# Layer 0 of a two-layer graph network: destination rows added to source rows by accumulating gathers into the message buffers

## What is computed

```python
s_n, v_n = _equiv_layernorm(s, v, gamma_s, beta_s, gamma_v)
src, dst = (edge_index[0], edge_index[1])
msg_s = (s_n @ Ws_src)[src] + (s_n @ Ws_dst)[dst]
msg_v = jnp.einsum('ncx,cd->ndx', v_n, Wv_src)[src] + jnp.einsum('ncx,cd->ndx', v_n, Wv_dst)[dst]
y0, y1 = (rsh[:, 0], rsh[:, 1:4])
w1 = rbf @ W_rbf
m1_s, m1_v = _cg_tp(msg_s, msg_v, y0, y1, w1[:, :CS], ...)
a = (m1_s @ W_alpha).reshape(e, H, AS_)
...
agg = jax.ops.segment_sum(alpha * h, dst, num_segments=n)
```

## Time and profile before

| what | value |
|---|---|
| median of 3 runs | 10095.94 us (10092.63 to 10127.31) |
| span of the profiled execution, first to last instruction | 8679.9 us |
| median less this span | 1416.0 us |
| layer 0's edge loop in the trace, from its first gather | 301 to about 6050 us |
| its regular groups (all but the first three and the last 26) | 380 to 5468 us |

### The profile page before, as it was taken

The page is one execution under the profiler, slowest core; times in us unless marked ns, Lnnn a source line. Parts: engine busy times, 40 slices in busy tenths (PEclk is TensorE's granted clock), DMA queues, the critical chain, the costliest instruction groups (busy, mean ns, idle before and its releaser), DMA issues. The chain is left out here.

```text
span 8679.9 us, 218293 instructions
## 1 busy us (share of the span) xinstructions
PE 7627.6 (88%) x60373; PEld 5771.5 (66%) x60374; DVE 7274.4 (84%) x17597; ACT 3252.4 (37%) x8375; POOL 6016.9 (69%) x5890
## 2 busy tenths in 40 slices
PE   2599999999999999999999999887968888888888
PEld 1487777877877787877787778776644444444445
DVE  4699999999999999999999999775368888888886
ACT  1244444444444444444444444332222222222223
POOL 0477777777777777777777777651037777777774
PEclk9799999999999999999999999987569999999999
DMA  4344444444444444444444444321012222222222
GB/s 53 78 101 99 102 100 101 102 100 101 101 102 101 101 101 99 102 100 100 100 101 102 101 102 100 77 75 29 11 37 67 67 67 67 67 67 67 67 67 61
DMA packets 616622, 725.52 MB, mean 84 GB/s; under 512 B 284132, under 2 KB 390884, under 8 KB 616573
## 3 DMA queue, kind: packets, MB, share of 16 engines
q0 software_dynamic: 225408, 385.00, 20.4%
q1 hardware_dynamic: 391165, 339.92, 15.3%
HBM read 708.40 MB, written 16.06 MB: 83 GB/s over the span
## 5 line engine op out<-in xcount | busy, mean ns | idle before, releaser
L778 PE MATMUL bank_pair<-w_msg,blocks 128*128 128x160 f32 (+2 forms) x15640 | 2078.7, 288 | 126.8 <-DVE blocks L1030 98.2
L720 POOL DMA_INDIRECT got_src<-src_tab,idx x1564 | 1661.5, 1062 | 659.4 <-POOL idx L714 358.5
L778 PEld LDWEIGHTS bank_pair<-w_msg,blocks 128*128 128x128 f32 x15640 | 1972.7, 192 | 218.5 <-DVE blocks L1030 218.5
L1504 POOL DMA_INDIRECT gotf<-f_tab,idx x1568 | 1702.3, 1086 | 514.2 <-issue 477.4
L720 POOL DMA_INDIRECT got_dst<-dst_tab,idx x1564 | 1486.3, 950 | 528.7 <-issue 503.7
L802 PEld LDWEIGHTS bank_pair<-weights_t,product 128*128 128x128 f32 x12896 | 1498.7, 195 | 309.9 <-issue 295.6
L802 PE MATMUL bank_pair<-weights_t,product 128*128 128x128 f32 x12896 | 1575.5, 281 | 9.5 <-ACT weights_t L932 8.2
L1545 PE MATMUL bank_pair<-val,to_node 128*128 128x385 f32 x3136 | 1247.6, 545 | 5.0 <-DVE val L1659 5.0
L1600 ACT ACTIVATE val<-pre,y_edge 128x160 f32<-128x160 f32 x1568 | 542.8, 417 | 1534.0 <-DVE pre L1640 1531.4
L1545 PEld LDWEIGHTS bank_pair<-val,to_node 128*128 128x128 f32 x3136 | 621.6, 208 | 536.8 <-issue 270.1
L767 PE MATMUL bank_pair<-edge,w_edge 64*128 64x512 f32 x3128 | 884.8, 642 | 9.5 <-DVE blocks L1030 9.5
(11 more groups left out here) (268 smaller groups left out, 11950.3 us busy)
## 6 DMA issues: line engine op xcount, KB each, us to landing
rbf<-in_rbf SPq DMA_DIRECT2D x391, 256.0 KB
dst_bc<-in_dst_rows SPq DMA_DIRECT2D x391, 256.0 KB
y<-in_y SPq DMA_DIRECT2D x391, 128.0 KB
y<-in_y SPq DMA_DIRECT2D x391, 96.0 KB
gotf<-f_tab,idx POOLq DMA_INDIRECT x1568, 2.7
got_src<-src_tab,idx POOLq DMA_INDIRECT x1564
got_dst<-dst_tab,idx POOLq DMA_INDIRECT x1564
rbf<-in_rbf SPq DMA_DIRECT2D x392, 32.0 KB, 1.7
```

The source lines that it names most:

```text
L720: pool.indirect_dma_start(out=buf[slot][:, t, :], out_offset=None, in_=table[:, :], in_offset=bass.IndirectOffsetOnAxis(ap=idx[slot][:, c: ...
L778: return nc.tensor.matmul(to, blocks[rows, k, P * t:P * t + P], w_msg[rows, c0:c1], start=start, stop=stop)
L1504: pool.indirect_dma_start(out=got[k][:, t, :], out_offset=None, in_=f_tab[:, :], in_offset=bass.IndirectOffsetOnAxis(ap=idx[k][:, t:t + 1] ...
```

## The change

The two pairs of gather buffers, POOL's add and its semaphore `summed` are gone. The gathers of the source rows write straight into `msg`. When all four of a group have landed (64 counts of `got`), four gathers of the destination rows follow, with `compute_op` add, so that the DMA engines add what they fetch to what `msg` holds. POOL's step g now does all of this for group g + 2, and `scale_edge(g + 2)` comes behind it. PE waits for all eight gathers (128 counts of `got`) where it waited for `summed`.

```diff
--- before.py
+++ after.py
@@ -505,6 +505,11 @@
     return use if slot == 1 else use - 1
 
 
+def next_use(slot, use):
+
+    return use if slot == 0 else use + 1
+
+
 def group_of(ap, g):
 
     return ap[g] if isinstance(g, int) else ap[bass.ds(g, 1)].squeeze(0)
@@ -514,7 +519,7 @@
         "ident", "iota_col", "least_bc", "idx_all", "w_edge", "w_msg", "w_val", "adot", "psum", "src_tab", "dst_tab",
         "peak", "sums"))
     s = {n: ctx.enter_context(nc.semaphore("l0_" + n)) for n in (
-        "edge0", "edge1", "edge_y0", "edge_y1", "dst0", "dst1", "got0", "got1", "indexed", "summed", "scaled",
+        "edge0", "edge1", "edge_y0", "edge_y1", "dst0", "dst1", "got0", "got1", "indexed", "scaled",
         "turned", "turned_copied", "weighed", "block_done", "message", "message_s", "tanh", "scalars", "leaky", "vector",
         "gated", "logit", "logit_step", "logit_wide", "geometry", "product", "scaled_y", "sum_copied", "projected",
         "far", "logit_turned", "top", "highest", "shifted", "peak_kept", "rescale", "weights", "factors",
@@ -604,8 +609,6 @@
                     chain.end()
 
         idx = [tmp(f"idx{i}", [P, 2 * TILES], I32) for i in range(2)]
-        got_src = [tmp(f"got_src{i}", [P, TILES, D]) for i in range(2)]
-        got_dst = [tmp(f"got_dst{i}", [P, TILES, D]) for i in range(2)]
         msg = [tmp(f"msg{i}", [P, TILES, D]) for i in range(2)]
         edge = [tmp(f"edge{i}", [P, GE]) for i in range(2)]
         y_edge = [tmp(f"y_edge0{i}", [P, TILES, 5]) for i in range(2)]
@@ -714,20 +717,19 @@
                     pool.tensor_copy(idx[slot][:], idx_all[:, bass.ds(g, 1), :].rearrange("p a c -> p (a c)")).then_inc(s["indexed"], 1)
                     wait(s["indexed"], g + 1)
 
-                def gather(slot, tiles):
-                    for t in tiles:
-                        for buf, table, c in ((got_src, src_tab, t), (got_dst, dst_tab, TILES + t)):
-                            pool.indirect_dma_start(
-                                out=buf[slot][:, t, :], out_offset=None, in_=table[:, :],
-                                in_offset=bass.IndirectOffsetOnAxis(ap=idx[slot][:, c:c + 1], axis=0)
-                            ).then_inc(s[f"got{slot}"], 16)
-
-                def add_message(g, slot, use, first):
-                    wait(s[f"got{slot}"], use * 128 + 128)
-                    if not first:
-                        wait(s["turned"], g * 2 - 2)
-                        wait(s["weighed"], g * 4 - 5)
-                    pool.tensor_tensor(msg[slot][:], got_src[slot][:], got_dst[slot][:], ALU.add).then_inc(s["summed"], 1)
+                def gather(slot, table, first, op):
+                    for t in range(TILES):
+                        pool.indirect_dma_start(
+                            out=msg[slot][:, t, :], out_offset=None, in_=table[:, :],
+                            in_offset=bass.IndirectOffsetOnAxis(ap=idx[slot][:, first + t:first + t + 1], axis=0), compute_op=op
+                        ).then_inc(s[f"got{slot}"], 16)
+
+                def take_sources(slot):
+                    gather(slot, src_tab, 0, ALU.bypass)
+
+                def add_targets(slot, use):
+                    wait(s[f"got{slot}"], use * 128 + 64)
+                    gather(slot, dst_tab, TILES, ALU.add)
 
                 def scale_edge(g, slot, use, first):
                     wait(s[f"edge{slot}"], use * 48 + 48)
@@ -739,25 +741,19 @@
                 def step(g, slot, use, now, mid, late):
                     if isinstance(g, int) and g + 2 >= NG:
                         return
-                    further = not (isinstance(g, int) and g + 4 >= NG)
-                    add_message(g + 2, slot, use + 1, False)
-                    if further:
-                        take_idx(g + 4, slot)
-                        wait(s["summed"], g + 3)
-                        gather(slot, (0, 1))
+                    wait(s[f"got{slot}"], use * 128 + 128)
+                    take_idx(g + 2, slot)
+                    wait(s["turned"], g * 2 + 2)
+                    take_sources(slot)
+                    add_targets(slot, use + 1)
                     scale_edge(g + 2, slot, use + 1, False)
-                    if further:
-                        gather(slot, (2, 3))
 
                 for first in range(2):
                     take_idx(first, first)
-                    gather(first, range(TILES))
+                    take_sources(first)
                 for first in range(2):
-                    add_message(first, first, 0, True)
+                    add_targets(first, 0)
                     scale_edge(first, first, 0, True)
-                    take_idx(first + 2, first)
-                    wait(s["summed"], first + 1)
-                    gather(first, range(TILES))
                 schedule(step, 2)(pool)
 
             @block.tensor
@@ -872,7 +868,7 @@
                     if now:
                         message_vectors(3).then_inc(s["message"], 1)
                     if now and not last_group(g):
-                        pe.wait_ge(s["summed"], g + 2)
+                        pe.wait_ge(s[f"got{other}"], next_use(slot, use) * 128 + 128)
                         if mid:
                             pe.wait_ge(s["top"], g)
                         else:
@@ -881,7 +877,7 @@
                         if mid:
                             pe.wait_ge(s["weights_copied"], g)
                         turn_message(other, 1)
-                pe.wait_ge(s["summed"], 1)
+                pe.wait_ge(s["got0"], 128)
                 turn_message(0, 0)
                 turn_message(0, 1)
                 schedule(step)(pe)
```

## The result

| | us, median | ratio to before, 95% interval |
|---|---|---|
| before | 10095.06 (10092.63 to 10127.31, 4 runs) | |
| changed | 11691.41 (11686.12 to 11708.22, 4 runs) | 1.1575 (1.1556 to 1.1594) |

The change costs 1596 us. The number forecast was 11005, the range 10300 to 11900. The time lies in the range, but in the part that the prediction gave to its rival of dear accumulating gathers.

What follows compares the result with a forecast made beforehand. TensorE and DVE were taken as the bound, POOL level with them. POOL's step would go from 14.09 to 16.62 us: +913 over 361 steps, -20 at the start, +15 at the end, +908, about 11005 us; range 10300 to 11900.

Steps and rivals of the forecast that it cites:

- rival of dear accumulating gathers: POOL's adding gathers cost 1.64 us each or delay the sources: step 19.1 us, 11910 us; chance 0.20 for above 11500.
- the landing becomes POOL's own time: POOL, between source and adding gathers: landing exposed at 3.5 us a step, ends 1.6 and 4.5, lengthened by SP's loads.
- the restart of 0.89: POOL after the landing: 0.89 us a step before the first adding gather, as after the copy of the indices.
- one that may join: The 256 KB dst_bc load may join SP's loads beside the source gathers and share the DMA engines.
- the low end taken from layer 1: Quiet landing behind the fourth source gather's row, from layer 1's same gather: 1.6 to 1.75 us.
- the sources and POOL's sum with copying gathers: POOL's step: four source gathers with gaps 4.92 us, the whole step 16.62 us with adding gathers priced as copying ones.
- DVE's line 998: Without POOL's add, DVE's line 998 falls to about 0.26 us on average, freeing 0.8 us of DVE a step.
- the accumulating gather taken at a copying one's price: POOL's adding gathers: 1.005 us each, four with gaps 4.92 us a step; the DMA engines' add priced at nothing.
- a mean over 1.2 us: Sign that the prediction is wrong: the adding gathers' mean on POOL is over 1.2 us.
- the base: Layer 0 step of the kernel before, taken from its first trace: 14.09 us.
- 1416 us around the span: Time outside the 8679.9 us span, taken from the median of the runs and kept beside a new span of about 9590.
- about 3 us before the transposes: TensorE waits for DMA or POOL ahead of its transposes, about 3 us a step, busy share 81% against 96%.

Runs made afterwards that it cites:

- the kernel of copying gathers: Changed kernel with plain destination gathers in place of adding ones, behind the same wait, the sum left out; 10455.82 us, ratio 1.0327.
- the second trace of the kernel before: The kernel before, unchanged, profiled a second time: span 10103.5 us at clock 0.878, 16.42 us a step; measured 10124.48 us, ratio 1.0011.
- the first execution: The kernel before, unchanged, in the trace that the prediction read: span 8679.9 us at an average granted clock of 0.947.
- the edge product in between: Changed kernel with POOL's edge product moved between the source gathers and the adding ones; SP's loads follow it; 10033.15 us, ratio 1.0067.
- second try with late loads: Changed kernel with SP's edge loads, and dst_bc behind them, waiting until the source gathers that POOL issues next have landed; 10362.48 us, ratio 1.0424.
- the accumulating kernel without the wait: Changed kernel with adding destination gathers into separate buffers that nobody reads, no wait for the sources, message the source row alone; 11761.09 us, ratio 1.1625.
- the three kernels of 11761 to 12443 us: Changed order without the wait, destination gathers into separate buffers: accumulating 11761.09 us; copying with POOL's add back 12102.89 us; copying without the sum 12442.46 us.
- 12916: Changed order with plain gathers into two buffer sets, no wait, no POOL add; TensorE sums by two accumulating matmuls per transpose; 12916.21 us, ratio 1.2963.

## Why the prediction came out as it did

**Right: the landing becomes POOL's own time.** The prediction had 4.39 us a step of landing and restart and wrote of 4.4 us as the sign. The changed kernel shows 450.2/97 = 4.64. That SP's loads make it long is shown, too: 4.64 us with them beside the sources, 2.39 with them behind. With the three edge loads beside the sources and `dst_bc` elsewhere, in the kernel of copying gathers, it is 3.1. So the larger part of the lengthening seems to come with `dst_bc`, which the prediction named as one that may join; that kernel has no adding gathers, and the two were not separated. Less the restart of 0.89, the 2.39 are 1.5 us of quiet landing, just under the low end taken from layer 1, 1.6 us.

**Right: the sources and POOL's sum with copying gathers.** Four sources with their gaps are 4 x 0.975 + 3 x 0.315 = 4.85 us, predicted 4.92. The kernel with the wait and without the accumulation goes at 17.4 us a step, of which POOL waits 0.9 us for PE; its own work is about 16.5, where the sum without dear adds, 16.62, stood.

**Right by luck: DVE's line 998.** It is L994 after; its group is 194 in 42.1 us, 259 ns, predicted 0.26. But the reason, that POOL's add is gone, doesn't hold for the timed runs. In the second trace of the kernel before, the add is still there and takes 1544 ns, and the line is as short (2000 to 4000 us):

```profile
L998 DVE SCALAR_TENSOR_TENSOR sums<-sums,factors,win_scaled 128x41 f32 x242 | 52.6, 259 | 28.2 <-DVE win_scaled L991 28.2
```

So the 0.8 us a step that DVE was to gain were there in the first execution only.

**Wrong: the accumulating gather taken at a copying one's price.** This is the step that failed. "The nearest row is that of the plain gather of the same 128 rows, and I take 1.005 us" put the four adds at 4.92 us. They are 4 x 1.927 + 3 x 0.305 = 8.6 us. An undisturbed one is 1.54 to 1.60, some 0.6 us over the copying one, or 2.2 to 2.4 us a step. The other 1.3 to 1.5 us are mostly the fourth of each step, 2.83 us on average, which runs beside DVE's L1049 to L1110. That lengthening isn't the accumulation's own: copying gathers in the same place, in the kernel with the wait, take up to 2.72 us, and 1.28 and 1.40 on average for the third and the fourth. The prediction named a mean over 1.2 us as the sign that it is wrong, and it is 1.93. The rival of dear gathers had the mechanism, with 1.64 us each and 11910 us for the time. The sum with the measured terms: 16.62 + 3.7 for the adds + 0.25 for the landing + 0.2 for the edge product and the copy of the indices (together 0.6 + 0.8 us longer, less the 1.2 that overlap in the rows) is 20.8 us, as measured.

**Wrong: the base.** 14.09 us a step is that of the first trace. The "1416 us around the span" that were added as a constant are not around it: in an execution like the timed ones layer 0 goes at 16.42 us a step, and the span of the changed kernel's profile is 11684.3 us at a median of 11691.41. The two errors pull apart: a base too low by 2.33 us makes the loss too large, a step after too low by 4.16 makes it too small, and 1.83 us x 361 = 660 us are most of the 688 between the 908 forecast and the 1596 measured. That the time lies in the range is luck to that extent: with the right base, the same step of 16.62 us would have given 0.2 x 361 = 72 us and a time under 10200, below the range. It follows as well that the kernel before has room on POOL in the timed runs, notwithstanding: in the second trace POOL's add and edge product wait 124.4/121 = 1.0 us a step for PE.

**The losses don't add.** Taking out SP's loads gives back 11.5 of the 15.75%, taking out the accumulation 12.5. Both kernels end near 17.4 us a step, but for different reasons. With the loads moved POOL has no slack, its 17.3 us are its own; without the accumulation POOL waits 0.9 us a step for PE, so more than POOL's work holds the step. The last 1 us goes when the edge product covers the landing: 16.42 us a step and 1.0067. That is within 1% of the kernel before; no variant was faster than it. It wasn't tried whether both cuts at once would come below 16.4.

**TensorE's waits and its clock.** PE waits before the transposes for the adding gathers, 120.8 us in 88 waits, 1.2 us a step, and longer for DVE's `blocks`, 301.9/97 = 3.1; the prediction had about 3 us before the transposes. PE's busy share is 3039/4000 = 76%, predicted 81. In the waits of the changed kernel:

```profile
DVE far L1065 <- DMA dst_bc<-in_dst_rows: 480.5, 96, 6.0
POOL msg L722 <- DMA msg<-src_tab,idx: 450.2, 97, 5.3
...
PE bank_pair L774 <- DVE blocks L1026: 301.9, 97, 4.0
```

DVE's 5 us for `dst_bc` are the same delay by another way, since that load stands behind `scaled` in SP's queue. The granted clock is 0.97 in the regular part with the edge product in between, 0.94 in the second trace of before, 0.93 in the second try with late loads, 0.88 in the changed kernel. It doesn't follow the busy time alone: the accumulating kernel without the wait has PE busy 3139 of 4000 us at 0.83, the changed one 3039 at 0.88. How much of the step the lower clock adds by itself was not separated; since POOL fills its step alone in the changed kernel, I take it for a consequence there rather than the cause.

**Open.** Why TensorE's matmuls stand apart by multiples of about 0.7 us where POOL is early and the edge product comes last (the three kernels of 11761 to 12443 us, and 12916), and why the kernel before loses 4.7% with its edge product last. Moving the edge product in between took most of the stalls away, 4.3 to 0.7 us a step, but moves SP's loads as well; the two were separated only in the changed kernel, which has no stalls. The stalls don't explain the 4.7%, since that kernel has 0.4 us of them a step. No cause is claimed. Open, too, is which of DVE's instructions lengthens a gather beside it.

## What to carry to other kernels

An accumulating gather saves an add on an engine, but it isn't free on the queue engine, and it brings a wait for a landing into an in-order instruction stream; put an independent instruction between the two sets of gathers, and look at what transfers that instruction's semaphore sets off. Here the same POOL work costs 15.8% or 0.7% by where one product stands, with the loads that follow it, and even at its best the change gains nothing. Before a sum is built on one trace, set its span beside the times: a span 14% below the median is another execution, not an overhead to be added.

## What the runs showed of the hardware

- With nothing beside it, an accumulating gather of 128 rows of 640 bytes takes POOL 1.54 to 1.60 us to issue, a copying one 0.94 to 1.01. q0 counts 375552 packets against 225408 on the page of the kernel before, for the same 385.00 MB.
- DVE's L1110, with two SBUF inputs, is lengthened from 0.43 to between 1.69 and 2.58 us where it overlaps POOL's edge product, and stays at 0.43 beside an adding gather alone (115 of 115 in the second try with late loads). The Trainium skill ("SBUF — State Buffer", section "Who interferes with whom") says that a DVE instruction with two SBUF inputs and a GpSimd one that reads SBUF contend, and the trace agrees: L1110 ends 0.3 us behind the edge product in all 96 overlaps of the changed kernel.
- Gathers of both kinds are lengthened in the stretch of DVE's L1049 to L1110: an adding one to as much as 3.29 us (changed kernel), a copying one to 2.72 us (the kernel with the wait and without the add).
- The kernel before ran once with a span of 8679.9 us (clock 0.947) and otherwise in 9924 to 10143 us (0.873 to 0.894): whole executions of one kernel can differ by 16%. The cause is open.
- Matmuls without any recorded wait stood 0.7 us or a multiple of it apart, in sum up to 4.3 us a step; in the step shown they begin at a granted clock of 1.00.
